# Query inverse norms as a per-row scale of the exponentials in a local-attention stack

## Reference, cut to what matters

```python
def attn_layer(x, Wqkv, qs, ksc, Wo):              # 16 heads of 64
    q, k, v = heads(x @ Wqkv)
    q = l2norm(q) * qs ;  k = l2norm(k) * ksc      # t / max(|t|, 1e-12)
    q = q * cos * scale + rotate_half(q) * sin * scale
    k = k * cos / scale + rotate_half(k) * sin / scale
    sim = einsum(q, k_window) * 8.0                # windows of 32, own and previous
    attn = softmax(where(mask, -inf, sim))
    return einsum(attn, v_window) @ Wo
```

## Time and profile before

| | us |
|---|---|
| median of 3 runs | 4347.09 |
| lowest, highest | 4330.38, 4347.27 |
| profiled execution, its own time | 4352.9 |
| its span in the trace | 4351.2 |
| busy TensorE, VectorE, ScalarE, GpSimd | 4027.8, 3345.6, 3100.0, 1798.7 |

### The profile page before, as it was taken

How to read it: one execution, slowest core, us unless ns; L and a number is a source line. 1 busy time by engine, 2 the same in 40 slices (tenths; PEclk the granted TensorE clock), 3 DMA queues, 4 the chain that set the end, 5 groups by cost and what they waited for, 6 DMA issues and landing times. The chain is left out here.

```text
span 4351.2 us, 113662 instructions
## 1 busy us (share of the span) xinstructions
PE 4027.8 (93%) x43857; PEld 2388.8 (55%) x43857; DVE 3345.6 (77%) x4981; ACT 3100.0 (71%) x7032; POOL 1798.7 (41%) x1071
## 2 busy tenths in 40 slices
PE   7997999999999999999967689999999999999998
PEld 3443555555555555555536545555555555555554
DVE  5774888888888888888735478888888888888885
ACT  3555777777777777777762267777777778777776
POOL 3111444444444444444404534444444444444442
PEclk7997999999999999999986589999999999999999
DMA  2212444444443443444300044444434444444342
GB/s 44 31 21 70 95 111 102 99 101 101 105 111 90 111 107 90 111 99 103 84 10 3 3 107 109 101 97 109 110 87 115 102 100 100 102 105 111 92 100 52
DMA packets 232520, 380.78 MB, mean 88 GB/s; under 512 B 59364, under 2 KB 122336, under 8 KB 231688
## 3 DMA queue, kind: packets, MB, share of 16 engines
q1 hardware_dynamic: 231560, 372.20, 36.9%
q10 hardware_dynamic: 384, 0.79, 0.1%
HBM read 39.22 MB, written 1.05 MB: 9 GB/s over the span
## 5 line engine op out<-in xcount | busy, mean ns | idle before, releaser
L835 POOL TENSOR_TENSOR b_prob<-b_prob,b_rinv 128x768 f32<-128x768 f32 x384 | 564.3, 1469 | 1778.3 <-DVE b_rinv L1281 1778.3
L841 POOL TENSOR_TENSOR b_prc<-b_prc,b_sws 128x1024 f32<-128x1024 f32 x384 | 907.7, 2364 | 72.2 <-DMA b_sws<-b_prs 72.2
L1143 ACT ACTIVATE b_prob<-ps,b_nmx 128x96 f32<-128x96 f32 x3072 | 749.0, 363 | 0.0
L885 PEld LDWEIGHTS ps<-ident,b_prob 128*128 128x128 f32 x3072 | 367.9, 140 | 406.5 <-ACT b_pT L1079 232.8
L1216 DVE SCALAR_TENSOR_TENSOR b_prc<-ps,b_qks,b_rot 128x512 f32<-128x512 f32 x768 | 571.1, 744 | 14.0 <-ACT b_sq L1104 13.3
L1218 DVE SCALAR_TENSOR_TENSOR b_prs<-ps,b_qks,b_rot 128x512 f32<-128x512 f32 x768 | 570.1, 742 | 0.0
L885 PE MATMUL ps<-ident,b_prob 128*128 128x128 f32 x3072 | 513.0, 281 | 46.5 <-DVE b_kr L1264 37.1
L1262 DVE TENSOR_TENSOR b_prc<-b_prc,ps 128x512 f32<-128x512 f32 x384 | 263.6, 686 | 369.9 <-PE ps L950 288.3
L1079 ACT ACTIVATE b_pT<-ps 128x512 f32<-128x512 f32 x724 | 435.5, 601 | 154.1 <-PE ps L885 151.1
L987 PE MATMUL ps<-b_wqkv,b_xs 128*128 128x256 f32 x1536 | 435.0, 406 | 2.2 <-DVE b_prs L1218 2.2
L938 PE MATMUL ps<-b_xs,b_wqkv 128*128 128x512 f32 x768 | 408.9, 614 | 23.3 <-issue 10.0
(11 more groups left out here) (293 smaller groups left out, 7218.0 us busy)
## 6 DMA issues: line engine op xcount, KB each, us to landing
b_sws<-b_prs SPq DMA_DIRECT2D x1536, 128.0 KB, 2.3
b_vs<-b_va SPq DMA_DIRECT2D x384, 256.0 KB, 3.8
b_wqkv<-in_L_ffn_Wqkv SPq DMA_DIRECT2D x96, 192.0 KB, 3.6
b_xs<-y SPq DMA_DIRECT2D x126, 128.0 KB, 2.3
b_wo<-in_L_ffn_Wo SPq DMA_DIRECT2D x96, 64.0 KB, 3.1
b_xs<-y SPq DMA_DIRECT2D x42, 127.8 KB, 2.4
b_rot<-in_rot SPq DMA_DIRECT2D x2, 2048.0 KB, 7.8
b_w<-in_L_ffn_W SPq DMA_DIRECT2D x24, 170.5 KB
```

The costliest lines, as they stand in the source:

```text
L835: pool.tensor_tensor(prob[:, r, :, P - KEYS:P], prob[:, r, :, P - KEYS:P], rinv[:, r % 2, :].rearrange("p (b a) -> p b a", a=1).broadcast_ ...
L841: pool.tensor_tensor(prc[:, r, :, :], prc[:, r, :, :], sws[:, r % 2, :, :], ALU.add)\
L885: t = pe.transpose(bank[6][:, i * P:(i + 1) * P], prob[:, kd, 4 * e + 2 * h + m, :], ident[:, :])
L1143: g = act.activation(prob[:, kb, i, P - KEYS:P], wide[0][:, e * CH + m * KEYS:e * CH + (m + 1) * KEYS], ACT.Exp, bias=nmx[:, kb % 2, i:i + 1])
```

## The change

It removes the spread of the query's inverse norms (L947) and the multiplication of the rotated query by it (L1262). The scores are then made of the unnormalised query. `take` keeps its two key patterns only. A new constant `pick` (128 x 4) takes the query's sums: in even slots, once for two units, four products with a 128-column piece of `rsp` as the stationary operand and `pick` as the moving one give the inverse norms (times 8) with tokens on the partitions, in 16 columns of bank 2. VectorE copies them into `rqs`. After the row maximum VectorE multiplies it by the row's inverse norm into `nmb`, and each exponential gets two operands per row, `nmb` as bias and a column of `rqs` as scale. Waits: VectorE waits for the four products and for its own maximum; the strips wait for the copy instead of the query's multiplication. One small constant is loaded more for each stack, with one more copy.

```diff
-        take = sb("take", [P, 4, P], F32R)
+        take = sb("take", [P, 2, P], F32R)
+        pick = sb("pick", [P, 4], F32R)
...
+        nmb = sb("nmb", [P, 2, NB])
+        rqs = sb("rqs", [P, 2, 2, NB])
...
                 def strips(U, b, pe=pe):
                     pe.wait_ge(S["sqk_done"], ONE + U + 1)
                     if b:
-                        pe.wait_ge(S["qn_done"], ONE + um(b)[0] + 1)
+                        pe.wait_ge(S["rq_cp"], ONE + twos(b) + 1)
...
                         pe.wait_ge(S["kn_done"], ONE + UB)
-                        pe.matmul(bank[2][:, :], take[:, 2 * (kb % 2), :], rsp[:, :], start=True, stop=True)
                         if d:
                             pe.wait_ge(S["y_add"], ONE + UD)
-                        pe.matmul(bank[3][:, :], take[:, 2 * (kb % 2) + 1, :], rsp[:, :], start=True, stop=True)\
-                            .then_inc(S["nb_mm"], 1)
+                        pe.matmul(bank[3][:, :], take[:, kb % 2, :], rsp[:, :], start=True, stop=True).then_inc(S["nb_mm"], 1)
+                        if kb % 2 == 0:
+                            for m in range(4):
+                                t = pe.matmul(bank[2][:, 4 * m:4 * m + 4], rsp[:, m * P:(m + 1) * P], pick[:, :], start=True, stop=True)
+                            t.then_inc(S["rq_mm"], 1)
...
                             g = act.activation(prob[:, kb, i, P - KEYS:P], wide[0][:, e * CH + m * KEYS:e * CH + (m + 1) * KEYS],
-                                               ACT.Exp, bias=nmx[:, kb % 2, i:i + 1])
+                                               ACT.Exp, bias=nmb[:, kb % 2, i:i + 1], scale=rqs[:, kb // 2, kb % 2, i:i + 1])
...
                         dve.wait_ge(S["nb_mm"], ONE + UB + 1)
-                        dve.tensor_tensor(prc[:, kb, 0, :], prc[:, kb, 0, :], bank[2][:, :], ALU.mult).then_inc(S["qn_done"], 1)
                         at = PAD + (kb % 2) * CH
                         dve.tensor_tensor(kr[:, at:at + CH], prc[:, kb, 1, :], bank[3][:, :], ALU.mult).then_inc(S["kn_done"], 1)
+                        if kb % 2 == 0:
+                            dve.wait_ge(S["rq_mm"], ONE + twos(b) + 1)
+                            dve.tensor_copy(rqs[:, kb // 2, :, :].rearrange("p r (e m) -> p r e m", e=2),
+                                            bank[2][:, 0:16].rearrange("p (m r e) -> p r e m", m=4, r=2)).then_inc(S["rq_cp"], 1)
...
-                        dve.tensor_reduce(nmx[:, kb % 2, :], sc, AX.X, ALU.max, negate=True).then_inc(S["smax_done"], 1)
+                        dve.tensor_reduce(nmx[:, kb % 2, :], sc, AX.X, ALU.max, negate=True).then_inc(S["nm_done"], 1)
+                        dve.wait_ge(S["rq_cp"], ONE + twos(b) + 1)
+                        dve.wait_ge(S["nm_done"], ONE + UB + 1)
+                        dve.tensor_tensor(nmb[:, kb % 2, :], nmx[:, kb % 2, :], rqs[:, kb // 2, kb % 2, :], ALU.mult)\
+                            .then_inc(S["smax_done"], 1)
```

More of the change, by code:

```diff
@@ L620, in stack_semaphores @@
             s_mm t_mm pv_mm wo_mm sqq_done sqk_done ln_done hi_done rn_done split_done va_cp exp_done
-            pt_cp o_cp pq_done pk_done swap_ld add_done qn_done kn_done smax_done
+            pt_cp o_cp pq_done pk_done swap_ld add_done rq_mm rq_cp kn_done nm_done smax_done
             ssum_done rinv_done pn_done y_add xin_done fin_done
@@ L741, in _ @@
                 for dst, src in ((rot[:, :, :], c["rot"]), (band[:, :, :], c["band"]), (head_of[:, :], c["head_of"]),
-                                 (prs[:, 0, 0, :].rearrange("p (s f) -> p s f", s=4), c["take"]),
+                                 (prs[:, 0, 0, 0:2 * P].rearrange("p (s f) -> p s f", s=2), c["take"]),
+                                 (prs[:, 0, 0, 2 * P:2 * P + 4], c["pick"]),
                                  (minus_hi[:, :], c["minus_hi"])):
@@ L852, in _ @@
                 ln_pe(pe, ln_call, lambda k: xT[:, cs(k)])
-                pe.wait_ge(S["const_ld"], ONE + 80 * (rep + 1))
-                pe.wait_ge(S["take_set"], ONE + rep + 1)
+                pe.wait_ge(S["const_ld"], ONE + 96 * (rep + 1))
+                pe.wait_ge(S["take_set"], ONE + 2 * (rep + 1))
                 def key_bank_free(u, pe=pe):
@@ L1033, in _ @@
                     pe.matmul(bank[end_mean[n]], jmean[:, :], xs[:, cs(2 + n)], start=True, stop=True).then_inc(S["f_mean"], 1)
-                pe.wait_ge(S["qn_done"], ONE + UALL)
+                pe.wait_ge(S["rq_cp"], ONE + PER // 2 * (L0 + DEPTH))
                 pe.wait_ge(S["exp_done"], ONE + UALL)
@@ L1205, in _ @@
                 ln_dve(dve, ln_call, lambda k: xT[:, cs(k)], lambda k: y[:, cs(k)], each=shift)
-                dve.wait_ge(S["const_ld"], ONE + 80 * (rep + 1))
-                dve.tensor_copy(take[:, :, :], prs[:, 0, 0, :].rearrange("p (s f) -> p s f", s=4)).then_inc(S["take_set"], 1)
+                dve.wait_ge(S["const_ld"], ONE + 96 * (rep + 1))
+                dve.tensor_copy(take[:, :, :], prs[:, 0, 0, 0:2 * P].rearrange("p (s f) -> p s f", s=2)).then_inc(S["take_set"], 1)
+                dve.tensor_copy(pick[:, :], prs[:, 0, 0, 2 * P:2 * P + 4]).then_inc(S["take_set"], 1)
                 dve.wait_ge(norm_done, NC * (ln_call + 1))
-                dve.wait_ge(S["take_set"], ONE + rep + 1)
+                dve.wait_ge(S["take_set"], ONE + 2 * (rep + 1))
                 dve.wait_ge(S["ld"], ONE + 64 * (rep + 1))
@@ L2077, in constants @@
     t["head_of"] = (row // DH == np.arange(32)[None, :] % 2).astype(np.float32)
-    t["take"] = np.stack([((row // 32 == s) & (row % 32 < 4) & (row % 2 == col // DH)) * (1.0, QK_SCALE)[s % 2 == 0]
-                          for s in range(4)], 1).astype(np.float32).copy()
+    t["take"] = np.stack([(row // 32 == s) & (row % 32 < 4) & (row % 2 == col // DH)
+                          for s in (1, 3)], 1).astype(np.float32).copy()
+    t["pick"] = np.concatenate([((row // 32 == s) & (row % 32 < 4) & (row % 2 == np.arange(2)[None, :])) * QK_SCALE
+                                for s in (0, 2)], 1).astype(np.float32)
     t["minus_hi"] = np.where(np.arange(P)[:, None] % 4 < 2, 0.0, -1.0).astype(np.float32)
```

## The result

| | before | after |
|---|---|---|
| median of four, us | 4342.61 | 4557.77 |
| ratio, with 95% interval | | 1.0498 (1.0477 to 1.0519) |
| span of the profiled execution | 4351.2 | 4559.5 |
| mean slot in the first stack | 9.18 | 9.73 |

What follows compares the result with a forecast made beforehand. TensorE was taken to bound slots 2, 4 to 6, 10 to 12; elsewhere ScalarE or VectorE comes last. Slot terms summed to 3.4 us a half, 24 halves, +82: 4347 + 82 = 4429 us; range from A (4322, a little below) to 4500.

Steps and rivals of the forecast that it cites:

- the price of VectorE's product: VectorE, every slot: the new 128 x 8 product after the maximum was priced like reciprocal L1281, 203 ns.
- "Nothing" for the maximum's way to ScalarE: Maximum reaches ScalarE 0.2 us later, but the exponentials stand behind L1133, which ends later: no cost.
- ScalarE's price: Exponentials: a second per-row operand costs 0.09 us each, +0.72 us a slot, 276 us of ScalarE's time.
- the prediction's sum: Sixteen slots of a half: 1.33 - 0.48 + 0.6 + 0.9 + 1.05 = 3.4 us; 24 halves, +82 us.
- The Gelu slots: Slots 7 and 13: `kr` comes 0.6 us earlier, but ScalarE's chain delays L1079; together +0.9 us a half.
- The variance slots: Slots 3 and 9: the wait for L1218 goes, but ScalarE's copy comes 0.4 us later; together +0.6 a half.
- The expectation of +95 us: For the scale of ones: slots without feed-forward, with Gelu and with variance do not absorb the delay; 24 x 4.0, about 4440.
- TensorE's part: TensorE: the key's spread saves 0.24 us a slot, four products cost 0.43; even slots +0.19, odd slots -0.24.
- B: Rival: ScalarE's delay is absorbed nowhere; 8 us a half, +192, 4540 us; chance 0.13.
- A: Rival: the exponentials' second operand costs nothing; -1.05 us a half, -25 us, 4322; chance 0.16.
- C: Rival: second operand near 20 to 30 ns, or slots 0, 1, 15 gain back more; about 4347; chance 0.09.
- the weak part of A: Rival A (second operand free) not in full, leaving the time within 0.5%; with C the chance is 0.12.

Runs made afterwards that it cites:

- scale of ones: Kernel before with one edit: each exponential gets a per-row scale operand, a column of ones; 4391.0 us, ratio 1.0129.
- after, maximum in PSUM: Changed kernel with the row maximum written into free columns of its score bank in PSUM instead of SBUF; 4408.5 us, ratio 1.0154.
- after, maximum in PSUM, no scale: Changed kernel with the row maximum in PSUM and exponentials without scale operand, leaving the query's norm out of the scores; 4316.0 us, ratio 0.9939.
- the kernel before (666 - 168): Kernel before plus a VectorE product of the row maximum with ones, both in SBUF, as the exponentials' bias; 4409.9 us, ratio 1.0161.

## Why the prediction was wrong, point by point

**The step that failed** is the price of VectorE's product: "a product of 128 x 8 that waits for the maximum just before it; the reciprocal L1281 has that size and that position, 203 ns". It has the size and the position, but one SBUF input, and the product has two. It measured 1139 ns, of which 168 are its own; the rest is the wait for a GpSimd instruction that reads SBUF. Rows with the right kinds of operand were in the trace: the split, L1240 and L1230, has two SBUF inputs and takes 741 to 1799 and 741 to 2831 ns at one size. The prediction takes it for its place in the order only. The effect is 149 us, some 36 of them by TensorE's clock, which the prediction kept at 1.00; without it the changed kernel takes 4408.5, within 21 us of the 4429 forecast. "Nothing" for the maximum's way to ScalarE fell with it: ScalarE waits 42.2 us for the product.

**ScalarE's price was right**: 0.09 us more per exponential forecast, 0.092 measured by starts; 2.6 to 2.7 us for eight forecast, 2.68 measured. That the price of a first operand, 0.08 by the rows of the prediction, holds for a second was a choice, and the scale of ones bears it out.

**What ScalarE's price costs the kernel was mis-sized.** Mean lengths of the slots over the halves, in us, summed over each pair, because the four products move time from odd slots to even ones. A slot is measured from the start of the maximum before it to the start of its own, so what happens behind the maximum of slot 7 counts to slot 8. The last row is the prediction's sum by the same pairs.

| slots | 0, 1 | 2, 3 | 4, 5 | 6, 7 | 8, 9 | 10, 11 | 12, 13 | 14, 15 |
|---|---|---|---|---|---|---|---|---|
| before | 17.15 | 18.21 | 18.54 | 17.39 | 20.54 | 18.57 | 17.37 | 18.97 |
| after | 19.17 | 19.80 | 18.94 | 17.94 | 21.99 | 18.81 | 18.01 | 20.91 |
| after, maximum in PSUM | 17.25 | 18.10 | 18.63 | 16.96 | 21.74 | 18.63 | 16.96 | 20.56 |
| after, maximum in PSUM, no scale | 16.99 | 17.70 | 18.57 | 16.93 | 20.35 | 18.57 | 16.90 | 19.35 |
| before, scale of ones | 17.21 | 18.12 | 18.71 | 17.38 | 21.06 | 18.71 | 17.37 | 19.95 |
| forecast of the change | +0.35 | +0.49 | -0.05 | +0.64 | +0.49 | -0.05 | +0.64 | +0.89 |

With the maximum in PSUM a half is 2.1 us longer, where the sum had 3.4; the two stacks are 51 us longer, against 82. Slots 4, 5, 10 and 11, bound by TensorE, stay within 0.1, as forecast. Slots 0 and 1 pay 0.1 instead of 0.35, and slots 2 and 3 are 0.1 shorter instead of 0.49 longer. The Gelu slots pay behind their maximum, so they are to be read with the pair that follows: slots 6 to 9 pay 0.8 where the sum had 1.1, slots 12 to 15 pay 1.2 where it had 1.5.

The two rows with the maximum in PSUM differ by the scale operand alone, 3.5 us a half. Taken slot by slot it costs 0.6 to 0.7 us in each of the slots 1, 3, 8, 9, 14 and 15, close to what the sum had for them, but slots 0 and 2 give back 0.4 and 0.3, which the sum did not have: a part of the delay is caught up in the slot behind. In the kernel before the scale of ones costs 1.8 us a half, of which the slots behind Gelu pay 0.5 and 0.7, as expected. The variance slots pay nothing there and slots 1 and 15 only 0.3 each. The expectation of +95 us was nearly twice the 52 measured: I had let each delay of a copy pass to the end of its slot.

**TensorE's part was right.** The four products in slot 2:

```profile
1205.23 0.50 PE L956 MATMUL ps<-b_pick,b_rsp 128*128 128x4 f32 x4
```

One lasts 230 ns, so the starts lie (0.50 - 0.23) / 3 = 0.09 apart, a little under the 0.11 forecast. L1264's wait at the second turn is gone as forecast: TensorE's idle time for it was 37.1 us, and with the maximum in PSUM the line of L889 has it at 1.0. The variance's wait for L1218 is halved where the forecast had it gone: 55.6 us before, 24.3 with the maximum in PSUM. VectorE's saving and the exchange on TensorE, without the two costs, are worth 27 us.

**The rivals.** B's number came nearest and its mechanism was not there: ScalarE's delay is absorbed in most slots. A's sum is within 2 us of the kernel that it describes, -27 against -25, but that is in part luck: by pairs it is off by up to 0.5 us (slots 6, 7, 12 and 13 gain 0.5 each pair where it had nothing, slots 14 and 15 lose 0.4), and the errors cancel. The two ways of sharing out the chances differ by 0.01: C and the weak part of A make 0.09 + 0.02, forecast and B 0.75. The rival that came true, that the instruction put in VectorE's place is slower than the one removed, was not in the list; the range was too narrow because its bounds for that product took in only rows with other operands.

## What to carry to other kernels

Price a new VectorE instruction by a row with the same memories for its inputs, not the same size alone, and look at the shortest and longest duration of that row: a spread at one size points to a wait inside the duration, which no idle time shows. A small product of two SBUF operands beside a busy GpSimd can cost more than a 128 x 512 one with one operand in PSUM (1139 against 686 ns here); free columns of a PSUM bank were enough to take the wait away. Ask also what a wait of some 2 us does to TensorE's clock. A second operand per row cost ScalarE 0.092 us, as much as 110 columns of data here: L533 starts 0.49 us apart with 512 columns and 0.17 with 128, or 0.83 ns a column. What such a delay costs the kernel depends on the slots in which ScalarE comes last: of 280 us 52 reached the time in one kernel and 92 in the other.

## What the runs showed of the hardware

- VectorE's product of two SBUF inputs waited for a running GpSimd instruction of 1.47, 2.35 or 3.44 us and ended 0.02 us after it; with one input in PSUM it took 166 to 169 ns all 384 times, 373 of them beside a running GpSimd instruction. The 128 x 512 split behaves so too: 741 to 1799 ns with two SBUF inputs, 736 to 748 with one.
- A second operand per row costs an activation 0.092 us of ScalarE, from start to start: eight of 96 columns take 1.95 us with a bias or a scale and 2.68 with both.
- TensorE's granted clock can fall to 0.50 behind a wait of about 2 us; a slot of 9.61 us is then 11.18. It did so 24 times in the stacks of the changed kernel and once with the maximum in PSUM.
- Making VectorE faster made its next collision worse: the product was held 0.50 us on average in the kernel before (666 - 168) and 0.97 in the changed one (1139 - 168). VectorE now waited for scores while GpSimd went on to its longer instruction, which the product met 116 times instead of once.
